# Window attention and displaced blur: output transpose moved to the attention bank, values after the second scores, shift folded into the blur matrix

## The reference

```python
x = x + L0(_gn(x), w_qkv, w_proj, b_proj, bias_table, rel_index)   # windows 7x7, 12 heads of 16
x = x + L1(_gn(x), offset)                                         # 8 positions, 24 channels each
```

## Time and profile before

| what | value |
|---|---|
| runs | 6381.01, 6397.56, 6429.35 us |
| median | 6397.56 us |
| the profiled execution | 6416.5 us, of which the span of instructions is 6414.7 us |
| busy: PE, DVE, ACT, POOL | 87%, 67%, 60%, 62% |
| mean granted TensorE clock | 0.893 |
| DMA in all | 790.17 MB, 1371147 packets |

### The profile page before, as it was taken

One profiled execution on the slowest core, in us unless ns is written; L12 is line 12 of the kernel. 1 busy time (PEld: TensorE's weight loads), 2 busy tenths in 40 slices (PEclk: granted clock), 3 DMA queues, 4 the chain that ended last, 5 costly groups with the idle time before them and its releaser, 6 DMA issues. The chain is left out here.

```text
span 6414.7 us, 256829 instructions
## 1 busy us (share of the span) xinstructions
PE 5579.4 (87%) x97860; PEld 4640.6 (72%) x97860; DVE 4304.0 (67%) x9677; ACT 3830.3 (60%) x8451; POOL 3961.2 (62%) x4452
## 2 busy tenths in 40 slices
PE   5998888888888888888888889888898888988895
PEld 4777777777777777777777777777777777777774
DVE  4666666676676666666766766766666666766663
ACT  2665656665566656666665666665666655666562
POOL 1566556666567665666665566665566656666665
PEclk9888988998899988889998899999899889899986
DMA  3455565555654555655565655565555556545553
GB/s 82 107 129 128 125 132 121 121 124 131 132 126 115 127 129 123 135 122 118 130 134 127 130 122 123 128 134 131 128 125 123 123 130 134 129 117 125 128 115 68
DMA packets 1371147, 790.17 MB, mean 123 GB/s; under 512 B 1184840, under 2 KB 1234312, under 8 KB 1365768
## 3 DMA queue, kind: packets, MB, share of 16 engines
q1 hardware_dynamic: 1369992, 773.90, 54.9%
HBM read 156.97 MB, written 154.14 MB: 48 GB/s over the span
## 5 line engine op out<-in xcount | busy, mean ns | idle before, releaser
L1185 POOL TENSOR_TENSOR probl<-prob,probh 98x588 f16<-98x588 f32 x1024 | 1349.2, 1318 | 349.4 <-DVE probh L1029 250.2
L1191 POOL TENSOR_TENSOR o<-osb,o 128x192 f16<-128x192 f32 x1024 | 601.0, 587 | 1449.9 <-ACT o L830 1418.0
L629 PE MATMUL pO<-vv,probh 98*49 98x34 f16 x24576 | 1019.9, 224 | 74.0 <-issue 59.9
L629 PEld LDWEIGHTS pO<-vv,probh 98*49 98x49 f16 x24576 | 868.7, 122 | 248.6 <-issue 223.1
L629 PE MATMUL pO<-vv,probl 98*49 98x34 f16 x12288 | 989.2, 228 | 2.0 <-issue 2.0
L822 ACT ACTIVATE mov<-pT 12x98 f16<-12x98 f32 x1024 | 247.8, 242 | 999.5 <-PE pT L596 996.4
L1014 DVE TENSOR_REDUCE mx<-pS 128x12 f32<-128x588 f32 x1024 | 778.1, 760 | 33.9 <-issue 16.1
L614 PE MATMUL pT<-qst,kst 96*98 96x49 f16 x12288 | 776.5, 210 | 25.6 <-issue 25.6
L817 ACT ACTIVATE prob<-pT 98x588 f32<-98x588 f32 x1024 | 673.1, 657 | 188.0 <-PE pT L614 180.8
L629 PEld LDWEIGHTS pO<-vv,probl 98*49 98x49 f16 x12288 | 774.9, 122 | 0.0
L1029 DVE CAST probh<-prob 98x588 f16<-98x588 f32 x1024 | 600.6, 587 | 225.6 <-ACT prob L817 208.3
(11 more groups left out here) (184 smaller groups left out, 16645.6 us busy)
## 6 DMA issues: line engine op xcount, KB each, us to landing
kst<-kh SPq DMA_DIRECT2D x1536, 98.0 KB, 2.2
qst<-qh SPq DMA_DIRECT2D x1536, 49.0 KB, 2.0
qst<-mix SPq DMA_DIRECT2D x768, 98.0 KB, 2.6
kst<-mix SPq DMA_DIRECT2D x768, 98.0 KB, 2.2
vv<-cv SPq DMA_DIRECT2D x1024, 73.5 KB
xr<-x_scratch SPq DMA_DIRECT2D x128, 588.0 KB
out<-xr SPq DMA_DIRECT2D x256, 294.0 KB
x_scratch<-xm SPq DMA_DIRECT2D x128, 392.0 KB, 3.2
```

The source lines that it names most:

```text
L629: mm = pe.matmul(pO[64 * win:64 * win + NT, OW * hp:OW * hp + OW], b[0:98, p % 2, PW * hp + NT * win:PW * hp + NT * win + NT], vv[:, g % 2 ...
L1185: pool.tensor_tensor(probl[0:98, p % 2, :], prob[0:98, p % 2, :], probh[0:98, p % 2, :], ALU.subtract).then_inc(S["pl_p"], 1)
L1191: pool.tensor_tensor(o16[:, p % 2, C:2 * C], osb[:, p % 2, :], o16[:, p % 2, 0:C], ALU.subtract).then_inc(S["ol_p"], 1)
```

## The change

1. x1 is written to DRAM in the order in which the blur reads it (`(2, HW, CC, HW)` in place of `(C, TOK)`): each store becomes two, for even and odd channels, in runs of 56 elements (224 bytes), and the two reads (four DMAs) become one, with 112 rows of 5376 elements, ahead of the image loads.
2. The shift of the second group norm goes into the blur matrix. xr, xc and amat get two more rows (112 becomes 114), xr holds 1.0 in them, coef has one row set instead of two, and POOL's second instruction (L1228) is gone.
3. pX moves from pT to the free columns of pO, the bank that `attend` writes and DVE's `normalize` reads. `turn_out` stands after blur stage 0 and `qk`, right ahead of `shifted`, and first waits for `normalize` (`on_d`); `shifted` no longer waits for `turned_out`, but `attend` does. ACT's `turned_out` goes to the end of its step.
4. `values` goes from ahead of `qk` to after `shifted` and blur stage 1.
5. The four tail statistics of step 4 go to steps 26, 30, 2 and 4.

```diff
-        pX = pT[:, 0, 320:512].bitcast(F16).rearrange("p (b t) -> p b t", b=3)
+        pX = pO[:, 320:512].bitcast(F16).rearrange("p (b t) -> p b t", b=3)
...
-                sp.dma_start(scratch[0:CM, t], xm[:, par(i), t]).then_inc(S["x1_out"], 16)
-                sp.dma_start(scratch[CM:C, t], xt[64 * h:64 * h + 64, par(i), CHUNK * (k % 2):CHUNK * (k % 2) + CHUNK]
-                             ).then_inc(S["x1_out"], 16)
-
-            def read_x1(y0, y1):
-
-                v = scratch.rearrange("(c s) (y x) -> s y c x", s=2, x=HW)
+                y = slice(2 * WS * k, 2 * WS * k + 2 * WS)
                 for s in (0, 1):
-                    sp.dma_start(xr[HW * s + y0:HW * s + y1, :].rearrange("y (c x) -> y c x", x=HW),
-                                 v[s][y0:y1]).then_inc(S["xr_in"], 16)
+                    sp.dma_start(scratch[s, y, 0:CM // 2].rearrange("y c x -> c y x"),
+                                 xm[s::2, par(i), t].rearrange("c (y x) -> c y x", x=HW)).then_inc(S["x1_out"], 16)
+                    sp.dma_start(scratch[s, y, CM // 2:CC].rearrange("y c x -> c y x"),
+                                 xt[64 * h + s:64 * h + 64:2, par(i), CHUNK * (k % 2):CHUNK * (k % 2) + CHUNK]
+                                 .rearrange("c (y x) -> c y x", x=HW)).then_inc(S["x1_out"], 16)
+
+            def read_x1():
+
+                sp.dma_start(xr[0:SY, :], scratch.rearrange("s y c x -> (s y) (c x)")).then_inc(S["xr_in"], 16)
...
-                        read_x1(0, HW // 2)
+                        read_x1()
...
-                    if p == 6 and prev:
-                        read_x1(HW // 2, HW)
...
-                if due("ox_a", i, p - 2):
-                    pe.wait_ge(S["ox_a"], nth("ox_a", i, p - 2))
...
+                if due("ox_a", i, p - 1):
+                    pe.wait_ge(S["ox_a"], nth("ox_a", i, p - 1))
...
-                    for n, q in at(p, 3, prev, att, nxt):
-                        turn_out(i + n, q)
                     b = blur_step(p, 13, prev)
                     if b is not None:
                         blur(i - 1, b, 0)
-                    v = v_step(p, att, nxt)
...
-                    if v:
-                        values(i + v[0], v[1])
...
+                    for n, q in at(p, 2, prev, att, nxt):
+                        pe.wait_ge(S["on_d"], nth("on_d", i + n, q + 1))
+                    for n, q in at(p, 3, prev, att, nxt):
+                        turn_out(i + n, q)
                     if att:
                         shifted(i, p)
                     if b is not None:
                         blur(i - 1, b, 1)
+                    v = v_step(p, att, nxt)
...
+                    if v:
+                        values(i + v[0], v[1])
...
-                    for n, q in at(p, 3, prev, att, nxt):
-                        turned_out(i + n, q)
...
+                    for n, q in at(p, 3, prev, att, nxt):
+                        turned_out(i + n, q)
...
-                    if prev and p == 4:
-                        dve.wait_ge(S["x1_p"], nth("x1_p", i - 1, 16))
-                        for t in range(4):
+                    for n, t, on in ((0, 0, att and p == 26), (0, 1, att and p == 30), (-1, 2, prev and p == 2),
+                                     (-1, 3, prev and p == 4)):
+                        if on:
+                            dve.wait_ge(S["x1_p"], nth("x1_p", i + n, 2 * (t + 4) + 2))
                             dve.bn_stats(gst[1][:, 8 + t, :],
-                                         xt[:, par(i - 1), ROW * t:ROW * t + ROW]).then_inc(S["gn2_bn"], 1)
+                                         xt[:, par(i + n), ROW * t:ROW * t + ROW]).then_inc(S["gn2_bn"], 1)
...
-                        pool.tensor_tensor(v, src, spread(coef[:, 0, cols], HW), ALU.mult).then_inc(S["xcm_p"], 1)
-                        pool.wait_ge(S["xcm_p"], nth("xcm_p", i - 1, b + 1))
-                        pool.tensor_tensor(v, v, spread(coef[:, 1, cols], HW), ALU.add).then_inc(S["xcf_p"], 1)
+                        pool.tensor_tensor(v, src, spread(coef[:, cols], HW), ALU.mult).then_inc(S["xcf_p"], 1)
```

More of the change, by code:

```diff
@@ L56 @@
 SY = 2 * HW
+SX = SY + 2
 WSC = 256.0
@@ L74 @@
 _at = 0
-for _n, _w in (("ident", 128), ("gmm", 128), ("gtm", 128), ("gmt", 128), ("gtt", 128), ("lm", SY),
+for _n, _w in (("ident", 128), ("gmm", 128), ("gtm", 128), ("gmt", 128), ("gtt", 128), ("lma", SX), ("lmb", SX),
                ("sm", CM // 2), ("kmask", 2), ("tscale", 1), ("u0", HW), ("ys", 1), ("smask", 2),
-               ("taps", TAPS), ("iota", 2)):
+               ("taps", TAPS), ("iota", 2), ("ext", SX)):
     CF[_n] = (_at, _at + _w)
@@ L201, in build @@
         gnb = sb("gnb", [128, 2], F32)
-        coef = sb("coef", [SY, 2, CC], F32)
+        coef = sb("coef", [SX, CC], F32)
         cmain, ctail = (xcf[0:n, b, 0:n].rearrange("p (a c) -> p a c", a=2)
@@ L240, in build @@
             PER[n] = PAIRS
-        for n in ("xcm_p", "xcf_p", "xch_a", "xcl_p", "c1_pe", "z_act", "z_dve", "c2_pe", "y_dve"):
+        for n in ("xcf_p", "xch_a", "xcl_p", "c1_pe", "z_act", "z_dve", "c2_pe", "y_dve"):
             PER[n] = NB
@@ L515, in _ @@
                                        stop=(half == 1), skip_group_check=True)
+            mm.then_inc(S["setup_pe"], 1)
+            pe.wait_ge(S["setup"], SET_EXT)
+            for n, bank in enumerate((pV, pQ)):
+                mm = pe.matmul(bank[0:SX, 0:POS * HW], const("ext", SY),
+                               xr[0:SY, (2 + n) * POS * HW:(3 + n) * POS * HW], start=True, stop=True,
+                               skip_group_check=True)
             mm.then_inc(S["setup_pe"], 1)
@@ L689, in body @@
                         blur(i - 1, b, 0)
+                    if nxt and p == 14:
+                        pe.wait_ge(S["gn1_dve"], nth("gn1_dve", i + 1, 7))
+                    q = qk_step(p, att, nxt)
+                    if q:
+                        qk(i + q[0], q[1], q[2])
+                    for n, q in at(p, 2, prev, att, nxt):
+                        pe.wait_ge(S["on_d"], nth("on_d", i + n, q + 1))
+                    for n, q in at(p, 3, prev, att, nxt):
+                        turn_out(i + n, q)
+                    if att:
+                        shifted(i, p)
+                    if b is not None:
+                        blur(i - 1, b, 1)
                     v = v_step(p, att, nxt)
@@ L696, in body @@
                         values(i + v[0], v[1])
-                    if nxt and p == 14:
-                        pe.wait_ge(S["gn1_dve"], nth("gn1_dve", i + 1, 7))
-                    q = qk_step(p, att, nxt)
-                    if q:
-                        qk(i + q[0], q[1], q[2])
-                    if att:
-                        shifted(i, p)
-                    if b is not None:
-                        blur(i - 1, b, 1)
                     u = before(v_step, p, prev, att, nxt)
@@ L731, in body @@
                         pe.wait_ge(S["gn2_dve"], nth("gn2_dve", i - 1, 12))
-                        o = pM[0:SY, 0:2 * CC].rearrange("p (a c) -> p a c", a=2)
-                        pe.matmul(o[:, :, 0:CM // 2], const("lm"), cmain, start=True, stop=True,
-                                  skip_group_check=True)
-                        pe.matmul(o[:, :, CM // 2:CC], const("lm", CT), ctail, start=True, stop=True,
-                                  skip_group_check=True).then_inc(S["gn2_pe"], 1)
+                        for o, g, n in ((pM[0:SX, 0:CM // 2], cmain, CM), (pM[0:SX, CM // 2:CC], ctail, CT)):
+                            pe.matmul(o, const("lma", n), g[:, 0, :], start=True, stop=False, skip_group_check=True)
+                            mm = pe.matmul(o, const("lmb", n), g[:, 1, :], start=False, stop=True,
+                                           skip_group_check=True)
+                        mm.then_inc(S["gn2_pe"], 1)
             bodies(pe, body)
@@ L953, in _ @@
             then(dve.tensor_tensor(gauss, gauss, spread(inside, HW), ALU.mult))
-            for s in (0, 1):
-                v = slice(HW * s, HW * s + HW)
-                m = const("smask", SY)[:, s:s + 1]
-                then(dve.tensor_scalar(amat[:, 0, :, v], gauss, m, None, ALU.mult))
-                then(dve.scalar_tensor_tensor(out=amat[:, 1, :, v], in0=gauss, scalar=m,
-                                              in1=amat[:, 0, :, v], op0=ALU.mult, op1=ALU.subtract))
+            assert count[0] == SET_EXT, count
+            dve.wait_ge(S["setup_pe"], 2)
+            for n, bank in enumerate((pV, pQ)):
+                ext = bank[0:SX, 0:POS * HW].rearrange("p (a y) -> p a y", y=HW)
+                k = slice(POS * n, POS * n + POS)
+                for s in (0, 1):
+                    v = slice(HW * s, HW * s + HW)
+                    m = const("smask", SX)[:, s:s + 1]
+                    then(dve.tensor_scalar(amat[:, 0, k, v], ext, m, None, ALU.mult))
+                    then(dve.scalar_tensor_tensor(out=amat[:, 1, k, v], in0=ext, scalar=m,
```

(2 more changed lines are left out.)

51 lines of the change are left out of this document (26 added, 25 removed).

## The result

The changed kernel takes 6171.95 us (median of 4 runs, 6160.22 to 6182.25), the kernel before 6404.65 (4 runs, 6381.01 to 6429.35): ratio 0.9636, 95% interval 0.9592 to 0.9679. It is 3.6% faster; forecast were 6100 us and a range of 5930 to 6300.

What follows compares the result with a forecast made beforehand. PE bounds where its queue is unbroken; time above that sits in steps 2 to 6 and 10 to 14. Gains 3.4 + 5.9 + 0.5 - 1.3 + 0.8 make 9.3 us a pass; with head and tail, 6100 us forecast, range 5930 to 6300.

Steps and rivals of the forecast that it cites:

- steps 2 to 6: Block with the step 4 stall: 29.5 us against 32.92, a gain of 3.4 us a pass (0 to 5.6).
- steps 18 to 22: Block with z and xc in the chain to om: 30.3 us against 30.77, a gain of 0.5 a pass.
- Part 1, steps 10 to 14: POOL's 5.09 us wait for xr goes, or nearly; the block gains 5.9 us a pass (2 to 6.8).
- Part 2: Shift folded into the blur matrix: POOL's 758 ns saving counted within the blocks; set-up costs 3 us once.
- Part 3, waits for om: PE's project and attend wait for om behind norm and qk_hi: new waits of 1 to 2 us in steps 2, 10, 18, 26.
- The rival in which ACT and PE take turns: attend behind turned_out in 16 norm steps: 1.6 us each, 12 us more a pass, 6470 us; chance 0.08.
- Part 4: values behind the second scores: same matmuls, but 0.6 us lost in step 5, where values covered the maxima's way.
- The other steps: Steps outside the four counted blocks: POOL's and DVE's short waits shrink, a gain of 0.8 us a pass (0 to 1.5).
- Head and tail: Outside the 31 passes: the tail gains some 9 us of its 12.30 for xr, the head loses 3.
- The clock kept in full: Rival: PE keeps its clock without the long stalls and late om costs half, 6 us more gained a pass, 5920 us; chance 0.19.
- xr late: Rival: POOL still waits 2 to 4 us for xr, leaving about 1 us of steps 10 to 14's gain, 6255 us; chance 0.13.
- Nothing: Rival: the removed waits come back one by one at the next engine, 6397 us within 1%; chance 0.05.

Runs made afterwards that it cites:

- layout_only: The kernel before with x1 stored in four pieces in the blur's order and read back in one transfer: 6326.04 us, ratio 0.9891.
- read_paced: The changed kernel with its x1 read in quarters issued in steps 5, 7, 9 and 11, each after the last landed: 6095.18 us, ratio 0.9538.
- the order alone: The kernel before with the turned output in its own bank, its turn behind qk, and values behind the second scores: 6291.91 us, ratio 0.9818.
- stats_only: The kernel before with the four tail statistics spread over steps 26, 30, 2 and 4: 6408.09 us, ratio 0.9991.
- values_back: The changed kernel with values ahead of qk again, as in the kernel before: 6254.03 us, ratio 0.9752.
- before_longer_code: The kernel before with two PE waits written twice, in attend and turn_out, a pass 64 instructions longer: 6388.15 us, ratio 0.9979.
- own_row: The changed kernel with the first qk of a chunk waiting only for the one row it reads: 6149.75 us, ratio 0.96.
- om_before_qk: The changed kernel with turned_out on ACT between norm and qk_hi instead of behind both: 6174.68 us, ratio 0.9648.
- read_in_four: The changed kernel with its x1 read as four transfers issued together, one behind the other: 6169.73 us, ratio 0.9634.

## Why the prediction came out as it did

The sign and the range were right; of 9.3 us a pass forecast, 8.3 were measured. That the two lie so close is luck in good part: against the forecast, steps 2 to 6 fell short by 3.9 us, steps 10 to 14 gained 0.3 more, steps 18 to 22 0.2 less and steps 26 to 29 0.9 more, and the steps for which 0.8 us had been put down gave 2.6, as a gain of 4.4 and a loss of 3.6 that nobody had seen coming, and 1.8 in the rest.

**Part 1, steps 10 to 14: right in its mechanism.** Forecast was a gain of 5.9 us, 6.2 came. Step 11 takes 5.60 us on average, as worked out, POOL has no wait for xr in the passes, the read is released 6.3 us after the stores began (7 forecast) and lands 12.3 later (7.7 to 15). layout_only has 4.5 us of it by itself. The size is helped by the pass that was read: the 16th image was a short one (190.3 us from step 0 to 31, 194.5 on average), and its own steps 10 to 14 fell from 34.85 to 31.09 only. On average they took 36.72 and take 30.55, not the 28.9 of the sum: steps 12 to 14, counted as PE's work without a wait, were to take 4.9, 5.8 and 5.7 us and take 5.88, 6.56 and 6.45, with 0.64, 0.54 and 0.73 us of waits for DVE in them and a clock of 0.90 to 0.96. What the term left out is what else waits while 2352 KB are queued: PE's code and vv. In the 13th image PE stands in the middle of `attend`, whose inputs are all there:

```profile
2402.09 0.21 PE L637 MATMUL pO<-vv,probl 98*49 98x34 f16 x1 [2.17 <-issue]
```

and in the 16th it waits for vv, issued behind the read:

```profile
2964.19 0.28 PE L637 MATMUL pO<-vv,probh 98*49 98x34 f16 x4 [3.02 <-DMA vv<-cv]
```

That is the loss of 3.6 us in steps 8 and 9. By the traces 1.79 us of it are waits for issue in step 8 and 0.57 waits for vv in step 9; the rest goes with the clock of step 9, 0.81 instead of 1.00. The waits for issue end with a code block: in 24 of the 31 passes PE stands for 1.3 to 3.5 us in step 8, and each time it goes on 2.5 to 2.9 us after a block of queue 8 has started. read_paced changes only the read and the waits for it and gives 2.4 of the 3.6 us back, with no idle PE in step 8 and 0.78 us for issue in step 9, so the read is shown as the cause of those.

**Steps 2 to 6: mis-sized.** Forecast was a gain of 3.4 us (0 to 5.6), measured a loss of 0.5. Step 4 is 4.20 (forecast 4.0) and step 3 5.13 (5.1). But step 2 is 7.71, not 6.8 (1.76 us of waits for om and a clock of 0.90), and steps 5 and 6 are 7.26 and 8.31, not 5.1 and 6.3, at a clock of 0.63 and 0.71. The step that failed is "I keep a part of its cost, 2.2 us": taking the long stall of step 4 away did not keep the clock. By the runs the order alone costs 3.4 us here and the statistics give 2.7 to 3.0 back. What sets the clock in step 5 stays open. It is 0.69 to 0.79 in the three kernels in which step 0 runs at about 0.8 (before, layout_only, stats_only), and 0.50 to 0.65 in all with full clock there but values_back (0.78), among them before_longer_code (0.60), in which nothing but the 64 repeated waits in PE's code, and with them the jump, differs. own_row shows that the wait for xnt in step 6 costs that step its clock, not step 5.

**Part 2: small, and its set-up mis-sized.** The fold was counted within the blocks; it is worth 0.4% in all, and its set-up took 16 us and not 3 (see the head).

**Part 3, waits for om: right in place, wrong as a cost.** They stand in steps 2, 10, 18 and 26 with 1.76, 1.33, 1.60 and 1.51 us a pass (1 to 2 forecast). Steps 18 to 22 gain 0.35 us (0.5 forecast; but step 22 takes 6.80 us, not 5.3, with a wait of `qk` for xnt of 1.18), steps 26 to 29 lose 0.4 (1.3). om_before_qk removes four fifths of them and gains nothing. The rival in which ACT and PE take turns did not come; its prices were also too low as written: a gain of 9.3 us is used up by 0.6 us more in each of 16 steps, not 1.3, and 1.6 us in each, less the 4 counted, make 22 us a pass, not 12.

**Part 4: wrong.** Counted as 0.6 us lost in step 5 and nothing elsewhere. values_back shows 1.5 us lost in step 5 and more than that gained in steps 0, 1, 6, 7 and 14, in all 1.2%, as much as part 1 alone.

**The other steps: missed.** 0.8 us were forecast for all of them; steps 30 to 1 alone gained 4.4. Some 2.5 us of that are the shorter jump, which before_longer_code has by the length of PE's code alone, though there a pass kept 0.4 us of it by the medians. The rest is not split further.

**Head and tail.** The tail was to gain 9 us and the head to lose 3. From the rows of windows the head (to the first `turn` of the 31 passes) went from 293.84 to 303.19, 9.4 longer, and the tail from 109.8 to 104.5, 5.3 shorter. POOL still waits 10.9 us for xr in the tail; the wait there was 14.4 us, the longest of the 31 in the earlier trace rows. The head's term failed on part 2's set-up, counted as 3 us: the first `turn` of all comes at 143.2 to 145.2 us in every kernel with the fold and at 127.9 to 129.7 in every one without. Before, DVE made the blur matrix (amat) by itself while PE worked on the bias tables, and then waited for PE until 60.93 us. Now the matrix comes out of PE, behind those tables, and DVE's work on it and on the rows of ones in xr stands in the way of all that follows:

```profile
64.10 0.68 DVE L972 TENSOR_SCALAR amat<-pV,prob 114x448 f16<-114x448 f32 x1 [26.19 <-PE pQ L521]
...
70.99 4.54 DVE L975 MEMSET xr<- 18x5376 f32 x1 [1.18 <-issue]
```

DVE's next piece (L963, now L979) starts at 76.58 us, not 60.93. Of the 16 us the first image's steps give 7 back.

**The rivals.** The clock kept in full: no, 0.93. xr late: no. Nothing: no, but stats_only, read_in_four and om_before_qk are each a case of it.

## What to carry to other kernels

A wait for a transfer that lands at a time of its own is an account into which earlier gains are paid: the same statistics edit was worth nothing ahead of it and 0.8% once it was gone (and the other parts were in), so free the latest transfer first and try again what had failed. A large transfer should be cut into what the next few steps need and issued at their pace, since what comes after it is late, PE's code and the copies to vv here; cutting it without spreading it did nothing. And a matmul block with no haste is worth trying behind the last step of the longest chain through the other engines, where it may cover their way, rather than ahead of it: here that was worth 1.2%, though why the clock of two steps hung on it stays open.
